# A 32-chunk recommender tower on one core: one more rolled copy of h in PSUM, six split pairs of tiles a chunk instead of five

## The chip, the cores and the metric

The kernel runs on one core of one Trainium2 chip. The metric is the device time of one launch in microseconds; lower is better. The engines have these names in the profile: PE is TensorE (PEld its weight loads), DVE is VectorE, ACT is ScalarE, POOL is GpSimd and SP is SyncE, which here only issues DMAs.

## The reference

The inputs are 1024 rows of 32 ids and 16 dense values. Each id picks a row of 32 numbers from its own table, which gives `x` of shape (1024, 32 fields, 32). A compressed interaction network with three layers works on `x`:

```
for i, (W, b) in enumerate(zip(Ws, bs)):
    z = einsum('bhd,bmd,ohm->bod', h, x, W.reshape(O, H, F))
    z = relu(z + b[None, :, None])
    if i < n_layers - 1: h, direct = z[:, :O//2], z[:, O//2:]
    else:                direct = z
out = sum over d of concat(directs)
```

Layer 0 has h = x (32 by 32 pairs of fields, 128 outputs), layer 1 has 64 by 32 pairs and 128 outputs, layer 2 has 64 by 32 pairs and one output. The 129 sums and the 16 dense values then pass through a small network (145 to 512 to 256 to 1, relu between). Everything is float32.

## The kernel before

The 1024 by 32 columns (sample, d) are cut into 32 chunks of 1024 columns. For a layer, each product h[i] * x[j] is a row, and 128 such rows are one tile, which PE multiplies by a 128 by 128 block of the weights. To make a tile, DVE multiplies h by x rolled over the partitions (`x_roll`, four shifts) or h rolled by 16 partitions a step (`h_roll`, entry 0 is h, entries 1 to 3 are copies rolled by one, two, three steps, made by DMAs). Tiles are made in pairs (128 by 2048 elements), one DVE instruction a pair. Layer 1 has 16 tiles, eight pairs.

A tile reaches PE in one of two ways. A **whole** pair is multiplied as float32 (eight matmul records of 512 columns). A **split** pair goes as two float32r parts: DVE makes the raw product (`raw`), ACT rounds it (`prod_hi`), and the remainder `raw - prod_hi` (`prod_lo`) is made by DVE (`split_rest`) or GpSimd; PE then runs hi*hi, hi*lo and lo*hi (twelve records a pair). A split begins only when its remainder is there.

Per chunk c before, layer 0 of the next chunk has two whole pairs, here called **W0a** and **W0b** on DVE and **L0a** and **L0b** on PE. Layer 1 has three whole pairs (R from `h_roll` entry 1, L1b and L1c from h itself) and five split pairs: B0, B1, B2, B3 (h rolled by two and three against x shift 0 to 3) and A1 (h rolled by one against x shifts 2 and 3). GpSimd makes the remainders of B1 and B3 and, between them, eight gathers of table rows (an indirect DMA each) for the chunk three ahead. DVE makes the remainders of B0, A1 and B2.

Five further pieces per chunk: `product16` and `split_rest16` (DVE) and two matmuls on PE make layer 0's pairs of fields 16 apart; ACT puts relu on layer 0 (`relu0`) and on layer 1 (`relu1`); `layer2_u` (PE) and `layer2` (DVE) make layer 2's product, and every fourth chunk `layer2_sum` (PE) adds four of them; `sum_direct` (DVE) sums layer outputs.

`mlp_ps` is one PSUM tile of 1024 columns. ACT copies the next chunk's x into it (`copy_x`), which W0a and W0b read, then h (`copy_h0`), which L1b and L1c read. So those four DVE products read PSUM and SBUF; the others read SBUF twice.

The order on each engine is written out by hand in its `step`, and engines meet only at semaphores. The whole products use a ring of two buffers (`prod`): the product number n waits until PE has used number n - 2 (`whole` in the vector block):

```
wait(dve, prod_used, n - RING + 1)
```

PE's order before is L0a, B3 of the chunk before, L0b, R, the 16-apart matmuls, `layer2_u`, B0, L1b, B1, L1c, A1, (`layer2_sum`), B2. In SP's step, the loads of `x_roll` for chunk c wait until the slot, last used by chunk c - 2, is free, and the three rolls of h of chunk c - 1 (`roll_h`, two DMAs each) stand between the second and the third of those loads.

Of the kernel before, what the change touches and what calls it, by code (L numbers as in the profile page):

```python
# [31 lines left out]
P = 128  # L32
# [100 lines left out]
def build_tower(nc, gather_ids, row_base, table, w0, w0_swapped, w1_whole, w1_split, w2, b0, b1, b2,  # L133
                dense_t, wt1a, wt1b, bt1, wt2, bt2, wt3, out):
    with ExitStack() as ctx:
# [39 lines left out]
        x_part16 = sb("x_part16", [P, 2, PART])  # L175
# [11 lines left out]
        h2 = sb("h2", [P, 2, BANK])  # L187
# [12 lines left out]
        mlp1_hi = prod_hi[:, 0:2, :, :].rearrange("p s k n -> p (s k) n")  # L200
        mlp1_lo = prod_lo[:, 0:2, :, :].rearrange("p s k n -> p (s k) n")
        wt2_hi = w1_hi[:, 0:M1 * TOP2 // P, :].rearrange("p t n -> p (t n)").rearrange("p (k n) -> p k n", n=TOP2)
        wt2_lo = w1_lo[:, 0:M1 * TOP2 // P, :].rearrange("p t n -> p (t n)").rearrange("p (k n) -> p k n", n=TOP2)
        mlp2 = x_roll[:, 0, 0:M2, :]
        wt2_sb = x_roll[:, 0, M2, :].rearrange("p (k n) -> p k n", n=TOP2)
        top_a_hi, top_a_lo = [prod_hi[:, SPLIT_SLOT[A1], k, :] for k in range(2)]
        top_b_parts = prod_lo[:, SPLIT_SLOT[A1], 0, :]
        wt1a_hi, wt1a_lo = [prod_lo[:, SPLIT_SLOT[A1], 1, k * TOP1:(k + 1) * TOP1] for k in range(2)]
# [21 lines left out]
        x_part16_loaded = [sem(f"x_part16_loaded{s}") for s in range(2)]  # L230
# [29 lines left out]
        lo1_ready = sem("lo1_ready")  # L260
# [79 lines left out]
        def _(pool):  # L340
# [14 lines left out]
            def gather(c, u, group, part):  # L355
# [6 lines left out]
                for g in range(part * GATHERS // 2, (part + 1) * GATHERS // 2):  # L362
# [6 lines left out]
            def lo1(c):  # L369

                rounded = settled(pool, c * SPLIT1 + B1 + 1)
                behind = settled(pool, lo_count(c, B0))
                pool.wait_ge(hi_ready, rounded)
                pool.wait_ge(lo_ready, behind)
                nc.gpsimd.tensor_tensor(prod_lo[:, SPLIT_SLOT[B1], :, :], raw[:, RAW_SLOT[B1], :, :],  # L375
                                        prod_hi[:, SPLIT_SLOT[B1], :, :], ALU.subtract).then_inc(lo1_ready, 1)

            def lo3(c):

                rounded = settled(pool, c * SPLIT1 + B3 + 1)  # L380
                behind = settled(pool, lo_count(c, B2))
                pool.wait_ge(hi_ready, rounded)
                pool.wait_ge(lo_ready, behind)
                nc.gpsimd.tensor_tensor(prod_lo[:, SPLIT_SLOT[B3], :, :], raw[:, RAW_SLOT[B3], :, :],  # L384
                                        prod_hi[:, SPLIT_SLOT[B3], :, :], ALU.subtract).then_inc(lo3_ready, 1)

            def step(c, u, group):
# [6 lines left out]
                more = not isinstance(c, int) or c + ahead < CHUNKS  # L394
                if more:
                    if u == 1:
                        make_rows(group + 1)
                    gather(c + ahead, (u + ahead) % UNROLL, group if u == 0 else group + 1, 0)
                lo1(c)
                if more:  # L400
                    gather(c + ahead, (u + ahead) % UNROLL, group if u == 0 else group + 1, 1)

            make_rows(0)
            for c in range(UNROLL - 1):
                for part in range(2):
                    gather(c, c, 0, part)
# [3 lines left out]
        def _(sp):  # L410
# [9 lines left out]
            def roll_h(c, s):  # L420

                sp.wait_ge(h1_ready, 2 * (c + 1))
                for a in range(1, ROLLS):
# [17 lines left out]
            def load_x(c, u):  # L441
# [16 lines left out]
                if is_first(c):  # L458
                    load_part16(c, s)
                if not isinstance(c, int) or c != 1:  # L460
                    load_base(c)
                for b in range(ROLLS):

                    if reuses:
                        sp.wait_ge(*free[b])
# [3 lines left out]
                    if b == 1:  # L469
# [6 lines left out]
                        if not is_first(c):  # L476
                            load_part16(c, s)
# [16 lines left out]
            sp.dma_start(wt2_sb, wt2).then_inc(mlp_loaded, 16)  # L494

# [10 lines left out]
        def _(dve):  # L506
# [22 lines left out]
            def product16(c, u, group):  # L529
                s = u % 2  # L530

                dve.wait_ge(gather_done[u], (group + 1) * (16 * GATHERS))
                dve.wait_ge(x_part16_loaded[s], (c - s + 2) * 8)
                wait(dve, twice16_ready, c * 64)
                nc.vector.tensor_tensor(raw16[:, :], gathered[:, u, :], x_part16[:, s, :], ALU.mult
                                        ).then_inc(raw16_ready, 1)

            def products0(c, u, group):
# [22 lines left out]
                if not is_first(c):  # L561
                    product16(c, u, group)

# [642 lines left out]
```

## Time and profile before

| What | us |
|---|---|
| median of 3 runs (1127.32 to 1129.06) | 1128.2 |
| the profiled execution's own time | 1127.21 |
| its span, first to last instruction | 1125.4 |
| PE busy | 1086.0 |
| DVE busy | 1034.8 |
| POOL busy | 744.1 |
| ACT busy | 597.8 |

The mean granted TensorE clock is 0.995. Busy PE is not PE at its peak: the ends of its records are modelled and overlap the next record's start, so the distance between two starts is the better measure. The steady part of the run, chunk after chunk, is nearly all of the span, so the period of one chunk times about thirty is the time.

### The profile page before, as it was taken

To read this page: it belongs to the slowest core of one execution; us is meant where nothing else is said; L and a number is where in the kernel's file an instruction comes from. 1 tells how busy PE (TensorE), PEld (TensorE's weight loads), DVE (VectorE), ACT (ScalarE), POOL (GpSimd) and SP (SyncE) were. 2 spreads that over 40 slices of the span, in tenths; PEclk is the share of its full clock that TensorE was granted. 3 is DMA by queue.
4 is the path that set the end of the run, shared out by engine and by line. 5 is a ranking of instruction groups with operands and counts; after the bars stand their busy time and mean duration, and the time that the engine had idled before them with its cause. 6 is when DMAs were issued, how large, how long until landed. Compare 5 with 4: busy or idle time off the path is not lost.

```text
span 1125.4 us, 11475 instructions
## 1 busy us (share of the span) xinstructions
PE 1086.0 (97%) x3562; PEld 660.5 (59%) x3562; DVE 1034.8 (92%) x580; ACT 597.8 (53%) x517; POOL 744.1 (66%) x333
## 2 busy tenths in 40 slices
PE   3789999999999999999999999999999999999997
PEld 1355655666565666656666666656665666656665
DVE  1589999999999999999999999999999999999993
ACT  0156555545654555565455556555545655555545
POOL 6466767777787777768777777877777787743110
PEclk9899999999999999999999999999999999999999
DMA  6665454665544466554446555544566554455200
GB/s 203 206 166 147 141 144 132 177 174 153 149 147 135 129 177 176 166 143 138 141 128 171 176 155 161 141 134 127 169 176 168 148 142 145 131 153 145 78 0 1
DMA packets 73576, 162.97 MB, mean 145 GB/s; under 512 B 14785, under 2 KB 39874, under 8 KB 73554
## 3 DMA queue, kind: packets, MB, share of 16 engines
q1 hardware_dynamic: 52738, 147.57, 46.2%
q10 hardware_dynamic: 12624, 10.92, 3.0%
q0 software_dynamic: 8192, 4.21, 2.3%
q8 instruction: 11, 0.18, 0.1%
q14 instruction: 11, 0.09, 0.0%
HBM read 95.52 MB, written 8.39 MB: 92 GB/s over the span
## 4 chain that ended last, share of the span: by engine, by line
PE 86%; DVE 6%; issue 2%; ACT 1%; DMA 1%; another core or an unknown queue 1%; ACTq 1%; POOL 1%; SPq 0%; DVEq 0%; POOLq 0%
PE z_ps L723 84%; DVE raw L591 2%; PE u_ps L723 2%; DVE prod L527 2%; DVE prod_lo L597 2%; DMA twice<-raw 1%; POOL gathered L364 1%; ACTq L1016 0%; ACT prod_hi L1097 0%; ACT h_roll L1083 0%; PE mlp_ps L723 0%; ACT h L969 0%; DMA gathered<-in_table,rows_sb 0%; DMA base_sb<-in_row_base 0%
## 5 line engine op out<-in xcount | busy, mean ns | idle before, releaser
L723 PE MATMUL z_ps<-prod,w_sb 128*128 128x512 f32 x1280 | 575.6, 596 | 10.8 <-ACT direct L959 4.0
L364 POOL DMA_INDIRECT gathered<-in_table,rows_sb x256 | 454.1, 1774 | 73.9 <-issue 68.3
L723 PEld LDWEIGHTS z_ps<-prod,w_sb 128*128 128x128 f32 x1280 | 243.6, 191 | 273.4 <-issue 262.3
L986 ACT CAST prod_hi<-raw 128x2048 fp32r<-128x2048 f32 x160 | 305.2, 1908 | 180.0 <-DVE raw L591 179.3
L591 DVE TENSOR_TENSOR raw<-h_roll,x_roll 128x2048 f32<-128x2048 f32 x160 | 363.4, 2288 | 1.2
L527 DVE TENSOR_TENSOR prod<-mlp_ps,x_roll 128x2048 f32<-128x2048 f32 x124 | 279.6, 2285 | 8.5 <-issue 5.7
L723 PE MATMUL z_ps<-prod_hi,w_hi 128*128 128x512 f32 x648 | 249.0, 464 | 3.5 <-DVE prod_lo L597 3.1
L375 POOL TENSOR_TENSOR prod_lo<-raw,prod_hi 128x2048 fp32r<-128x2048 f32 x32 | 146.8, 4587 | 135.4 <-DVE prod_lo L597 109.1
L597 DVE TENSOR_TENSOR prod_lo<-raw,prod_hi 128x2048 fp32r<-128x2048 f32 x98 | 223.9, 2286 | 1.0
L384 POOL TENSOR_TENSOR prod_lo<-raw,prod_hi 128x2048 fp32r<-128x2048 f32 x30 | 139.0, 4632 | 122.3 <-DVE prod_lo L597 122.3
L723 PE MATMUL z_ps<-prod_lo,w_hi 128*128 128x512 f32 x648 | 204.8, 396 | 0.0
L723 PE MATMUL z_ps<-prod_hi,w_lo 128*128 128x512 f32 x648 | 204.2, 395 | 0.0
L723 PEld LDWEIGHTS z_ps<-prod_hi,w_hi 128*128 128x128 f32 x648 | 121.4, 189 | 72.9 <-issue 47.8
L723 PEld LDWEIGHTS z_ps<-prod_hi,w_lo 128*128 128x128 f32 x648 | 121.6, 188 | 30.1
L723 PEld LDWEIGHTS z_ps<-prod_lo,w_hi 128*128 128x128 f32 x648 | 121.6, 188 | 29.4
L955 ACT ACTIVATE h_roll<-z_ps,b_sb 64x1024 f32<-64x1024 f32 x64 | 71.2, 1112 | 95.3 <-PE z_ps L723 84.1
L999 ACT COPY mlp_ps<-h_roll 128x1024 f32<-128x1024 f32 x32 | 32.6, 1017 | 130.6 <-DVE prod L527 130.6
L527 DVE TENSOR_TENSOR prod<-h_roll,x_roll 128x2048 f32<-128x2048 f32 x32 | 73.3, 2292 | 27.7 <-PE z_ps L723 20.9
L969 ACT ACTIVATE h<-z_ps,b_sb 64x512 f32<-64x512 f32 x64 | 43.6, 682 | 26.4 <-PE z_ps L723 25.5
L959 ACT ACTIVATE direct<-z_ps,b_sb 64x1024 f32<-64x1024 f32 x32 | 35.6, 1111 | 33.0 <-DVE top_a L612 29.4
L612 DVE TENSOR_REDUCE top_a<-direct 128x1024 f32 (+1 forms) x32 | 38.7, 1209 | 0.0
L973 ACT ACTIVATE direct<-z_ps,b_sb 64x1024 f32<-64x1024 f32 x32 | 35.5, 1109 | 0.8
(71 smaller groups left out, 329.5 us busy)
## 6 DMA issues: line engine op xcount, KB each, us to landing
x_roll<-x_dram SPq DMA_DIRECT2D x128, 512.0 KB
x_base<-x_dram SPq DMA_DIRECT2D x32, 512.0 KB
h_roll<-h_roll SPq DMA_DIRECT2D x32, 448.0 KB
h_roll<-h_roll SPq DMA_DIRECT2D x32, 384.0 KB
h_roll<-h_roll SPq DMA_DIRECT2D x32, 320.0 KB, 6.0
x_dram<-gathered SPq DMA_DIRECT2D x64, 128.0 KB
twice<-raw ACTq DMA_DIRECT2D x128, 64.0 KB
h_roll<-h_roll SPq DMA_DIRECT2D x32, 192.0 KB, 7.0
```

The costliest lines, as they stand in the source:

```text
L364: nc.gpsimd.indirect_dma_start(gathered[:, u, g * DIM:(g + 1) * DIM], None, table, bass.IndirectOffsetOnAxis(ap=rows_sb[:, col:col + 1], a ...
L375: nc.gpsimd.tensor_tensor(prod_lo[:, SPLIT_SLOT[B1], :, :], raw[:, RAW_SLOT[B1], :, :], prod_hi[:, SPLIT_SLOT[B1], :, :], ALU.subtract).th ...
L384: nc.gpsimd.tensor_tensor(prod_lo[:, SPLIT_SLOT[B3], :, :], raw[:, RAW_SLOT[B3], :, :], prod_hi[:, SPLIT_SLOT[B3], :, :], ALU.subtract).th ...
L527: nc.vector.tensor_tensor(prod[:, slot % RING, :, :], in0, in1, ALU.mult).then_inc(prod_ready, 1)
L591: nc.vector.tensor_tensor(raw[:, RAW_SLOT[r], :, :], hs, xs, ALU.mult).then_inc(raw_ready, 1)
L597: nc.vector.tensor_tensor(prod_lo[:, slot, :, :], raw[:, RAW_SLOT[r], :, :], prod_hi[:, slot, :, :], ALU.subtract).then_inc(lo_ready, 1)
L612: nc.vector.tensor_reduce(sums[:, :, bass.ds(group * rows, rows)], direct[:, u % 2, :].rearrange("p (q r d) -> p q r d", q=QUADS, d=DIM), ...
L723: return nc.tensor.matmul(*args, **kw)
L955: nc.scalar.activation(h_roll[half * HID:(half + 1) * HID, s, 0, :], z0_ps[0:HID, :], ACT.Relu, bias=b0_sb[0:HID, :]).then_inc(h1_ready, 1)
L959: nc.scalar.activation(direct[0:HID, s, :], z0_ps[HID:P, :], ACT.Relu, bias=b0_sb[HID:P, :]).then_inc(direct0_ready, 1)
L969: nc.scalar.activation(h2[half * HID:(half + 1) * HID, s, :], z1_of(c)[0:HID, half * BANK:(half + 1) * BANK], ACT.Relu, bias=b1_sb[0:HID, ...
L986: nc.scalar.copy(prod_hi[:, SPLIT_SLOT[r], :, :], raw[:, RAW_SLOT[r], :, :]).then_inc(hi_ready, 1)
```

## The change

Layer 1 has now two whole pairs and six split pairs. The whole pair R becomes the split pair A10 (h rolled by one against x shifts 0 and 1); A1 is now named A12. ACT copies the h rolled by one into `mlp_ps` (`copy_h1`, after the two whole products of layer 1 have read h there), and A10 and A12 read it from PSUM. Both whole products of layer 1, here **L1a** and **L1b**, are those that read h in `mlp_ps`.

GpSimd now makes three remainders per chunk, B3 of the chunk before, B0 and B2, with two, three and three gathers behind them. Each waits for a point in DVE's order as well as for its data (`window`): B3 for the remainder of A12, B0 for `product16`, B2 for `split_rest16`. DVE makes the remainders of B1, A10 and A12. There are three raw buffers (`RAW_RING`) instead of two.

The orders are written anew. DVE, step c: W0a, W0b (of c + 1), B0, B1, `product16`, L1a, L1b, `sum_direct`, B2, remainder of B1, `split_rest16`, A10, A12, `layer2`, B3, remainder of A10, remainder of A12. PE: L0a, B3 of c - 1, L0b, L1a, L1b, B0, the 16-apart matmuls, `layer2_u`, B1, B2, A10, (`layer2_sum`), A12. ACT: `copy_h0`, round B0, `relu1`, the four DMAs of `double_pairs16`, round B1, `copy_h1`, `round_pairs16`, round B2, round A10, `relu0`, round A12, `copy_x`, round B3, `copy_late`. SP: the three rolls of h stand behind all four loads of `x_roll`, in the order two, three, one; the loads wait for the raw products A10, A10, A12 and B3 of the chunk that used the slot. `x_part16` and `h2` have one buffer each, and two weights of the last network are loaded at the end, by SP, into `x_roll`.

```diff
-WHOLE1 = 3
-B0, B1, A1, B2, B3 = range(5)
-SPLIT1 = 5
+WHOLE1 = 2
+B0, B1, B2, A10, A12, B3 = range(6)
+SPLIT1 = 6
 RING = 2
-SPLIT_SLOT = (0, 1, 2, 0, 1)
+SPLIT_SLOT = (0, 1, 2, 0, 1, 2)
-RAW_SLOT = (0, 1, 0, 1, 0)
-RAW_RING = 2
-LO_ORDER = {B0: 1, A1: 2, B2: 3, B3: 4}
+RAW_SLOT = (1, 2, 0, 1, 2, 0)
+RAW_RING = 3
+LO_ORDER = {B1: 1, A10: 2, A12: 3, B3: 4}
...
+            def lo(c, r, window, opened, ready):
+                rounded = settled(pool, c * SPLIT1 + r + 1)
+                opened = settled(pool, opened)
                 pool.wait_ge(hi_ready, rounded)
+                pool.wait_ge(window, opened)
+                nc.gpsimd.tensor_tensor(prod_lo[:, SPLIT_SLOT[r], :, :], raw[:, RAW_SLOT[r], :, :],
+                                        prod_hi[:, SPLIT_SLOT[r], :, :], ALU.subtract).then_inc(ready, 1)
...
-                    lo3(c - 1)
+                    lo(c - 1, B3, lo_ready, lo_count(c - 1, A12), lo3_ready)
+                    gather(*after, range(0, 2))
-                lo1(c)
+                    lo(c, B0, raw16_ready, c + 2, lo0_ready)
+                    gather(*after, range(2, 5))
+                    lo(c, B2, lo16_ready, c + 2, lo2_ready)
+                    gather(*after, range(5, GATHERS))
...
(SP, load_x)
+                    free = [settled(sp, (c - 2) * SPLIT1 + r + 1) for r in (A10, A10, A12, B3)]
...
-                        if reuses:
-                            roll_h(c - 1, 1 - s)
+                if reuses:
+                    roll_h(c - 1, 1 - s)
...
(DVE, split_product)
+                if r == A10:
+                    dve.wait_ge(h1_copied, c + 1)
+                    dve.wait_ge(lo0_ready, c + 1)
+                elif r == A12:
+                    dve.wait_ge(lo_ready, lo_count(c, B1))
+                elif r == B3:
+                    dve.wait_ge(lo2_ready, c + 1)
...
+                if r in (A10, A12):
+                    k = PAIR * (r - A10)
+                    hs, xs = twice(mlp_ps[:, :]), x_roll[:, s, k:k + PAIR, :]
...
(ACT)
+            def copy_h1(c, u):
+                s = u % 2
+                act.wait_ge(h1_rolled[s][0], (c - s + 2) * 16)
+                act.wait_ge(prod_ready, first1(c) + WHOLE1)
+                nc.scalar.copy(mlp_ps[:, :], h_roll[:, s, 1, :]).then_inc(h1_copied, 1)
...
-                act.wait_ge(prod_ready, first1(c - 2) + WHOLE1)
+                act.wait_ge(raw_ready, (c - 2) * SPLIT1 + A12 + 1)
                 nc.scalar.copy(mlp_ps[:, :], x_base[:, :]).then_inc(x_copied, 1)
```

## Rows read from the trace of the kernel before

**Rows 1.** The page's first part: engine, busy us (share of span), instructions.
```profile
PE 1086.0 (97%) x3562; PEld 660.5 (59%) x3562; DVE 1034.8 (92%) x580; ACT 597.8 (53%) x517; POOL 744.1 (66%) x333
```

**Rows 2.** Waits of DVE: engine and line, released by, us in total, times, longest.
```profile
DVE prod L527 <- PE z_ps L723: 21.5, 18, 5.4
```

**Rows 3.** Timeline of PE: start us, us, engine, line, operation, out<-in, shape, count.
```profile
676.81 1.03 PE L723 MATMUL z_ps<-prod_hi,w_hi 128*128 128x512 f32 x2
...
680.01 7.03 PE L723 MATMUL z_ps<-prod,w_sb 128*128 128x512 f32 x16
686.47 1.04 PE L723 MATMUL z_ps<-hi_lo,w_sb 128*128 128x512 f32 x2
...
703.49 0.62 PE L723 MATMUL z_ps<-prod_hi,w_hi 128*128 128x512 f32 x2
...
706.29 3.60 PE L723 MATMUL z_ps<-prod,w_sb 128*128 128x512 f32 x8
709.32 1.03 PE L723 MATMUL z_ps<-prod_hi,w_hi 128*128 128x512 f32 x2
```

**Rows 4.** Timeline of DVE over one chunk; brackets: idle before, and releaser.
```profile
689.61 1.21 DVE L612 TENSOR_REDUCE top_a<-direct 128x1024 f32 x1
...
701.87 4.60 DVE L527 TENSOR_TENSOR prod<-mlp_ps,x_roll 128x2048 f32<-128x2048 f32 x2
706.39 0.63 DVE L535 TENSOR_TENSOR raw<-gathered,x_part 128x256 f32<-128x256 f32 x1
...
709.92 2.29 DVE L527 TENSOR_TENSOR prod<-h_roll,x_roll 128x2048 f32<-128x2048 f32 x1 [0.70 <-issue]
...
714.45 0.69 DVE L568 TENSOR_TENSOR hi_lo<-twice,hi_lo 64x512 fp32r<-64x512 f32 x1
...
717.38 4.50 DVE L527 TENSOR_TENSOR prod<-mlp_ps,x_roll 128x2048 f32<-128x2048 f32 x2
721.79 0.41 DVE L605 TENSOR_TENSOR h2x<-u_ps,x_late 128x256 f32<-128x256 f32 x1
722.12 1.21 DVE L612 TENSOR_REDUCE top_a<-direct 128x1024 f32 x1
723.25 4.48 DVE L591 TENSOR_TENSOR raw<-h_roll,x_roll 128x2048 f32<-128x2048 f32 x2
```

**Rows 5.** Timeline of DVE: the sums of the outputs in steps 1 and 30.
```profile
100.63 1.21 DVE L612 TENSOR_REDUCE top_a<-direct 128x32 f32<-128x1024 f32 x1
...
1049.64 1.21 DVE L612 TENSOR_REDUCE top_a<-direct 128x32 f32<-128x1024 f32 x1
```

**Rows 6.** Timeline of DVE early on: a remainder that PE waits for.
```profile
76.15 2.28 DVE L597 TENSOR_TENSOR prod_lo<-raw,prod_hi 128x2048 fp32r<-128x2048 f32 x1
```

**Rows 7.** Timeline of PE there: the split that waited, and what follows it.
```profile
78.48 0.73 PE L723 MATMUL z_ps<-prod_hi,w_hi 128*128 128x512 f32 x2 [0.29 <-DVE prod_lo L597]
...
81.40 3.60 PE L723 MATMUL z_ps<-prod,w_sb 128*128 128x512 f32 x8
```

**Rows 8.** Timeline of ACT in the same chunk.
```profile
687.55 2.25 ACT L955 ACTIVATE h_roll<-z_ps,b_sb 64x1024 f32<-64x1024 f32 x2 [2.90 <-PE z_ps L723]
690.86 1.11 ACT L959 ACTIVATE direct<-z_ps,b_sb 64x1024 f32<-64x1024 f32 x1 [1.06 <-DVE top_a L612]
...
697.07 1.01 ACT L1005 COPY mlp_ps<-x_base 128x1024 f32<-128x1024 f32 x1
699.79 1.91 ACT L986 CAST prod_hi<-raw 128x2048 fp32r<-128x2048 f32 x1 [1.70 <-DVE raw L591]
```

**Rows 9.** Timeline of POOL: the two remainders of that stretch.
```profile
702.10 4.64 POOL L384 TENSOR_TENSOR prod_lo<-raw,prod_hi 128x2048 fp32r<-128x2048 f32 x1 [3.86 <-DVE prod_lo L597]
...
717.61 4.58 POOL L375 TENSOR_TENSOR prod_lo<-raw,prod_hi 128x2048 fp32r<-128x2048 f32 x1 [2.37 <-DVE prod_lo L597]
```

**Rows 10.** The rolls of h (line 425): issue to landing.
```profile
DMA to landing us min/median/max: 5.2/6.0/7.0
```

**Rows 11.** Busy time of a ten-us stretch with those rolls; last three: clock, DMA share, GB/s.
```profile
590.00:600.00 10.00, 10.00 (x36) 6.50 (x35) 9.96 (x7) 7.53 (x7) 8.87 (x5) 1.00 1.01 256
```

More of the change, by code:

```diff
@@ L229, in build_tower @@
         x_base_loaded = sem("x_base_loaded")
-        x_part16_loaded = [sem(f"x_part16_loaded{s}") for s in range(2)]
+        x_part16_loaded = sem("x_part16_loaded")
         x_roll_loaded = [[sem(f"x_roll_loaded{s}_{b}") for b in range(ROLLS)] for s in range(2)]
@@ L361, in gather @@
                 wait(pool, late_copied, freed)
-                for g in range(part * GATHERS // 2, (part + 1) * GATHERS // 2):
+                for g in columns:
                     col = u * GATHERS + g
@@ L391, in step @@
                 if not_first(c) and pool_makes_lo3(c - 1 if isinstance(c, int) else c):
-                    lo3(c - 1)
+                    lo(c - 1, B3, lo_ready, lo_count(c - 1, A12), lo3_ready)
                 ahead = UNROLL - 1
                 more = not isinstance(c, int) or c + ahead < CHUNKS
+                after = c + ahead, (u + ahead) % UNROLL, group if u == 0 else group + 1
                 if more:
@@ L422, in roll_h @@
                 sp.wait_ge(h1_ready, 2 * (c + 1))
-                for a in range(1, ROLLS):
+                for a in (2, 3, 1):
                     r = H_ROLL * a
@@ L628, in step @@
                 before = (u - 1) % UNROLL, group if u else group - 1
-                def rolled_once():
-                    dve.wait_ge(h1_ready, 2 * (c + 1))
-                    dve.wait_ge(h1_rolled[s][0], (c - s + 2) * 16)
-                    whole(first1(c), slot1(c, u), twice(h_roll[:, s, 1, :]), x_roll[:, s, 0:PAIR, :])
-                if is_first(c):
-                    rolled_once()
                 split_product(c, u, B0)
-                if not is_first(c):
-                    rolled_once()
                 split_product(c, u, B1)
                 if not is_last(c):
-                    split_rest16(c + 1)
-                split_rest(c, B0)
+                    product16(c + 1, (u + 1) % UNROLL, group if u < UNROLL - 1 else group + 1)
                 dve.wait_ge(h0_copied, c + 1)
                 for k in range(PAIRS0):
-                    whole(first1(c) + 1 + k, slot1(c, u) + 1 + k, twice(mlp_ps[:, :]),
+                    whole(first1(c) + k, slot1(c, u) + k, twice(mlp_ps[:, :]),
                           x_roll[:, s, k * PAIR:(k + 1) * PAIR, :])
                 if not_first(c):
+                    sum_direct(c - 1, *before)
+                split_product(c, u, B2)
+                split_rest(c, B1)
+                if not is_last(c):
+                    split_rest16(c + 1)
+                split_product(c, u, A10)
+                split_product(c, u, A12)
+                if not_first(c):
                     layer2(c - 1, *before)
-                    sum_direct(c - 1, *before)
-                split_product(c, u, A1)
-                split_product(c, u, B2)
-                split_rest(c, A1)
                 split_product(c, u, B3)
-                split_rest(c, B2)
+                split_rest(c, A10)
+                split_rest(c, A12)
                 if not pool_makes_lo3(c):
@@ L1027, in step @@
                     copy_h0(c, u)
+                round_products(c, B0)
+                if not_first(c):
+                    relu1(c - 1, (u - 1) % UNROLL)
                 if not is_last(c):
                     double_pairs16(c + 1)
-                round_products(c, B0)
+                round_products(c, B1)
+                copy_h1(c, u)
                 if not is_last(c):
                     round_pairs16(c + 1)
-                if not_first(c):
-                    relu1(c - 1, (u - 1) % UNROLL)
-                round_products(c, B1)
+                round_products(c, B2)
+                round_products(c, A10)
                 if not is_last(c):
                     relu0(c + 1, (u + 1) % UNROLL)
-                round_products(c, A1)
-                if not is_last(c):
-                    copy_late(c + 1, (u + 1) % UNROLL, group if u < UNROLL - 1 else group + 1)
-                round_products(c, B2)
+                round_products(c, A12)
                 if not isinstance(c, int) or c + 2 < CHUNKS:
@@ L1044, in step @@
                 round_products(c, B3)
+                if not is_last(c):
+                    copy_late(c + 1, (u + 1) % UNROLL, group if u < UNROLL - 1 else group + 1)
                 if u == 0 and not_first(c):
@@ L1160, in lay_out @@
     w1 = a["L0_rec_W1"].reshape(P, HID, FIELDS)
[L1161 to L1162 removed]
+    whole = [(0, 0), (0, 1), (0, 2), (0, 3)]
+    split = [(2, 0), (3, 0), (2, 1), (3, 1), (2, 2), (3, 2), (1, 0), (1, 1), (1, 2), (1, 3), (2, 3), (3, 3)]
     for name, tiles in (("w1_whole", whole), ("w1_split", split)):
```

142 lines of the change are left out of this document (62 added, 80 removed).

## The prediction

> **What bounds the kernel now.** I read the busy shares first: PE 97%, DVE 92%, the others far lower [rows 1]. So two engines are near full, and a gain on one is capped by the other. Next the timeline of PE in the middle of the run: each record starts before the one ahead has ended, with no idle time. Then DVE over the same chunk: it is full but for one gap before R, the whole product behind B0 [rows 4]. It is DVE that waits for PE there: L0a starts at 706.29 [rows 3], and R at 709.92 [rows 4], 3.63 us later, when PE gives the ring's buffer back; the waits by releaser say the same, 21.5 us in 18 such waits [rows 2]. PE is the bound. A chunk takes 32.51 us (722.12 - 689.61, rows 4); every fourth one has `layer2_sum` as well, and the mean over 29 periods is (1049.64 - 100.63)/29 = 32.72 [rows 5].
>
> **PE's own work.** A whole pair is priced from starts: L0b and R together take 6.46 us from start to start (680.01 to 686.47) and a single one ahead of a split 3.03 (706.29 to 709.32), so a further whole pair is worth 3.43; a further split pair is 2.80 (703.49 to 706.29) [rows 3]. One pair goes from whole to split, so PE saves 0.63 us a chunk, if nothing else ends later.
>
> **DVE's work.** It loses R and one remainder (GpSimd makes three now, not two) and gains the raw product A10 and the remainder of A10; A1 and B2 stay in other places. Thirteen instructions of 2048 columns before, thirteen after. A10 and A12 read PSUM in place of SBUF: two products with a PSUM input take 4.50, two with SBUF inputs 4.48 [rows 4]. So nothing is gained or lost in DVE's work, about 31.8 a chunk (32.51 less the gap of 0.70).
>
> **The loop that the new order closes.** L1b on DVE takes the ring's buffer that W0b filled, so it waits until PE has done L0b. In the old order the product behind L0b had 7 us of other work ahead of it; the one that waits sooner, R, waits only for L0a. In the new order PE reaches L0b only after A10, A12, L0a and B3, and A10 waits for the last remainder but one that DVE makes. This is one loop, once a chunk, and no engine can run ahead in it:
>
> DVE, from the start of L1b to the end of A10's remainder: L1b 2.21 (half of 4.41, 717.38 to 721.79), `sum_direct` 1.13 (722.12 to 723.25), B2 2.21, a remainder and `split_rest16` 2.93 (714.45 to 717.38), A10 and A12 4.41, `layer2` 0.33 (721.79 to 722.12), B3 2.21 [rows 4], the remainder 2.28 [rows 6]: 17.71.
>
> DVE to PE: the remainder that PE waited for ended at 76.15 + 2.28 = 78.43 [rows 6], and the split began at 78.48 [rows 7]: 0.05.
>
> PE, from A10 to the release of L1b: A10, a split that has waited, 2.92 (78.48 to 81.40) [rows 7]; A12 2.80; L0a 3.03; B3 behind it 3.20 (676.81 to 680.01); L0b until DVE goes on 3.63, as for R above [rows 3, 4]: 15.58.
>
> Sum 33.34. Inside it B3 on DVE also waits for GpSimd's remainder of B2, whose raw buffer it takes. That remainder starts 0.23 after the first of two products that read PSUM (717.38 on DVE, 717.61 on POOL) and takes 4.58 to 4.64, so it ends 4.81 to 4.87 after A10's start [rows 4, 9]; DVE is at B3 after 4.41 + 0.33 = 4.74. That adds 0.1 to 0.2: 33.5 us. The same loop in the old order, R to B2's remainder to B2, L0a and R, is 24.46 (32.51 less 8.05, the way from W0a to R in rows 4) + 0.05 + 2.92 + 3.63 = 31.06, and so had 1.45 to spare under 32.51.
>
> **The sum.** `layer2_sum` stands between A10 and A12 and so in the loop; it costs what it did, 0.21 a chunk on the mean (32.72 - 32.51). New mean 33.71, against 32.72: 0.99 a chunk. L1b waits for an L0b in steps 1 to 30, which makes 29 periods: 28.7 us. Against the profiled execution's 1127.2 that is 1155.9; the median of the runs lies 1.0 above that execution, so 1157. The first step and the end I leave at nothing: DVE makes the same number of instructions there, and the two weights now loaded late land long before the last network needs them. If that cover is gone they cost their own few us.
>
> **Edits that I cost at nothing.** ACT has one round more (1.91) and one copy more (1.01) a chunk [rows 8]; its 597.8 us of busy time [rows 1] rise by 32 x 2.92 = 93 to some 690, so there is room on the mean. Its order: round A10 is ready 10.76 + 1.91 = 12.7 after L1b's start, and DVE wants it at 15.4; `copy_h1` needs L1b's end and is wanted by A10 6.3 later, behind `sum_direct`, B2, a remainder and `split_rest16`. GpSimd: three remainders are 13.9 and eight gathers of 1.77 with 0.3 between them about 16.6, together 30.5 of 33.5. Without that cover, B3 on DVE waits longer and each us of it is a us of the loop. Loads of `x_roll` now start behind A10 and not behind L1b; the first has from there to W0a, about 10 us. The rolls of h, six DMAs, pass two loads on SP's queue and are priced under the rivals; the store of the next chunk's gathered rows, queued behind them, serves a chunk two steps ahead. With one `x_part16` its load waits for `product16` of the chunk before, a step earlier; with one `h2`, `relu1` waits for a `layer2_u` a step earlier: both are long past.
>
> **The port that DVE and GpSimd share.** The trace shows little of it: GpSimd's remainder ends at 702.10 + 4.64 = 706.74 [rows 9], and the small `product16`, with two SBUF inputs, started at 706.39, takes 0.63 instead of about 0.4 [rows 4]. The Trainium skill, in "SBUF — State Buffer", section "SBUF: two separate sides", says that a VectorE instruction with two SBUF inputs and a GpSimd instruction that reads SBUF exclude each other for the whole instruction. By that rule a late remainder of B3 on GpSimd would hold up B0 on DVE altogether; row and rule agree in direction, and how long a large product is held no row shows. This is a loop of its own, priced from rows: L1b to the end of A10 10.76; on ACT round A10 1.91, `relu0` 2.25 + 1.11, round A12 1.91, `copy_x` 1.01, round B3 1.91, together 10.10 [rows 8]; GpSimd 0.2 + 4.64 [rows 9]; DVE's B0, B1, `product16` and L1a 7.05: 32.75. It is shorter than 33.5, so it is not added.
>
> **The rivals.**
>
> *PE stays the bound.* The period would be 32.51 - 0.63 = 31.88, the mean 32.09, and the time 1127.2 - 0.63 x 29 = 1109. For it: PE is at 97%, DVE has 0.70 of slack, and the work of both fits. Against it: the loop is made only of waits that stand in the code and of durations in rows. It decides only if PE runs L0b more than 1.6 us sooner after A10's remainder than rows 3 and 7 show.
>
> *The loop through ACT and GpSimd sets the period, with the first loop shorter than I think.* Then 32.75 + 0.21 = 32.96, and 0.24 x 29 = 7 more: 1134. If both loops come out 0.3 shorter there is no change, 1128. For it: the exclusion above; against it: the first loop is longer by 0.75.
>
> *Something is late inside the loop, so that it is slower still.* Two candidates. ACT: if its row of five is 1 us longer than 10.10 plus the 0.75 in hand, or GpSimd comes late to B2's remainder because its three gathers run long. DMA: the rolls of h, behind all loads now, are wanted by B0. From A10's end six transfers of 0.52 MB and one of 0.13 must pass, at 256 GB/s with the DMA engines full [rows 11] 12.8 us; with the landing of a roll 6.0 (5.2 to 7.0) from its issue [rows 10] they come about 25 after L1b's start, and 25 + 7.05 = 32.1 against 33.5. Roughly 1 us more in the loop is 29 us: 1186; half that, 1171.
>
> **How the numbers follow.** The forecast, loop of 33.2 to 33.8: 1148 to 1166, chance 0.62. Something late inside: 1166 to 1190, 0.18. The second loop or a shorter first one: 1126 to 1148, 0.10, of which 0.04 within 0.2% (2.3 us, about what a measurement of this kernel can tell). PE the bound: 1105 to 1126, 0.10. So faster 0.10, same 0.04, slower 0.86. The range 1138 to 1182 leaves out the PE bound, half of the third case and the top of the second, about 0.18.
>
> **What would show it.** Right: DVE idles before L1b and not before R's place, released by PE, some 0.5 to 1.5 us a chunk; PE idles 1.2 to 1.6 us before A10, released by DVE's remainder (line 597 of before); the start of `sum_direct` repeats every 33.5 us. Wrong: PE without idle time before A10 means the loop is not closed; idle time of DVE before B3 (released by GpSimd) or before B0 (by a DMA) means the third rival; a large product on DVE beginning only when GpSimd's remainder ends would show the exclusion. The forecast falls if the period is under 33.

## The result, and the profile after

| | before | after |
|---|---|---|
| median of the runs, us | 1127.8 (4 runs, 1126.6 to 1129.1) | 1178.6 (4 runs, 1175.5 to 1181.3) |
| profiled execution, us | 1127.2 | 1175.5 |
| its span, us | 1125.4 | 1173.7 |
| mean granted TensorE clock | 0.995 | 0.989 |

The ratio is 1.045, with a 95% interval of 1.042 to 1.048: the change makes the kernel slower by 51 us. The forecast was 1157, and its range reached from 1138 to 1182. The sign and the place of the first loss are as forecast, and a second loss of some 20 us came on top, so that the time lies where the forecast's third rival put it (1166 to 1190).

The page's first part after (engine, busy us, share of the span, instructions), to be held against [rows 1]:

```profile
PE 1082.3 (92%) x3690; PEld 682.7 (58%) x3690; DVE 1036.8 (88%) x580; ACT 691.3 (59%) x581; POOL 921.1 (78%) x365
```

PE and DVE do what they did, within 4 us, in a span that is 48 us longer: neither has more to do, both wait more. (ACT and POOL have more to do, but are busy for 59% and 78% of the span.) For what PE and DVE wait is in the waits by releaser of the kernel after (engine, line, released by, us in total, times, longest). First DVE, the answer to [rows 2], then PE, and last the same wait of PE in the kernel before:

```profile
DVE raw L594 <- DMA h_roll<-h_roll: 39.6, 25, 3.7
DVE prod L530 <- PE z_ps L721: 12.0, 15, 1.1
...
PE z_ps L721 <- DVE prod_lo L600: 35.8, 30, 1.5
...
PE z_ps L723 <- DVE prod_lo L597: 3.1, 4, 1.6
```

PE now waits 1.2 us a chunk for a remainder of DVE (35.8 in 30), which before it did four times in the run. DVE waits for PE less often than before, and the largest entry is new: B0 waits for the rolls of h.

The timeline of DVE after, one chunk (start, us, operation; brackets: idle time before, and releaser), with the first and the thirtieth sum of outputs ahead of and behind it:

```profile
94.81 1.21 DVE L615 TENSOR_REDUCE top_a<-direct 128x32 f32<-128x1024 f32 x1
...
544.16 1.21 DVE L615 TENSOR_REDUCE top_a<-direct 128x1024 f32 x1
...
573.54 4.48 DVE L530 TENSOR_TENSOR prod<-mlp_ps,x_roll 128x2048 f32<-128x2048 f32 x2
577.94 1.21 DVE L615 TENSOR_REDUCE top_a<-direct 128x1024 f32 x1
...
584.30 4.49 DVE L594 TENSOR_TENSOR raw<-mlp_ps,x_roll 128x2048 f32<-128x2048 f32 x2
...
596.13 4.58 DVE L530 TENSOR_TENSOR prod<-mlp_ps,x_roll 128x2048 f32<-128x2048 f32 x2
...
603.00 4.49 DVE L594 TENSOR_TENSOR raw<-h_roll,x_roll 128x2048 f32<-128x2048 f32 x2 [2.28 <-DMA h_roll<-h_roll]
...
607.74 4.48 DVE L530 TENSOR_TENSOR prod<-mlp_ps,x_roll 128x2048 f32<-128x2048 f32 x2
612.14 1.21 DVE L615 TENSOR_REDUCE top_a<-direct 128x1024 f32 x1
...
1089.54 1.21 DVE L615 TENSOR_REDUCE top_a<-direct 128x32 f32<-128x1024 f32 x1
```

The mean over 29 periods is (1089.54 - 94.81)/29 = 34.30, against 32.72 in [rows 5]: 1.58 x 29 = 45.8 of the 48.3 us between the two profiled executions. The other 2.5 are the start (94.81 against 100.63, 5.8 sooner) and the end (1173.7 - 1089.54 = 84.2 against 75.8, 8.4 longer). Much of these two is only where the mark stands: `sum_direct` comes 16.0 behind W0a now (596.13 to 612.14) and came 20.25 behind it before (701.87 to 722.12) [rows 4]. Single periods are uneven: 33.78 (544.16 to 577.94), 34.20 (577.94 to 612.14); over the 29 they go from 33.46 to 35.44, and none is shorter. So there is a floor at the forecast's 33.5, and something that adds to it in most chunks.

What adds is the gap before B0. L1b starts at 573.54 + 2.24 = 575.78, the rolls are there at 603.00: 27.2 us later, where the forecast had 25. From B0 to the next L1b are 607.74 + 2.24 - 603.00 = 6.98, and 27.2 + 7.0 = 34.2 is this period.

PE of the same chunk, from the split A10 that waited (its first record, then those of A12, L0a, B3 and L0b):

```profile
593.63 0.73 PE L721 MATMUL z_ps<-prod_hi,w_hi 128*128 128x512 f32 x2 [0.90 <-DVE prod_lo L600]
...
596.54 0.62 PE L721 MATMUL z_ps<-prod_hi,w_hi 128*128 128x512 f32 x2
...
599.34 3.60 PE L721 MATMUL z_ps<-prod,w_sb 128*128 128x512 f32 x8
602.37 1.03 PE L721 MATMUL z_ps<-prod_hi,w_hi 128*128 128x512 f32 x2
...
605.57 3.59 PE L721 MATMUL z_ps<-prod,w_sb 128*128 128x512 f32 x8
```

The steps are 2.91, 2.80, 3.03 and 3.20: the forecast's terms to 0.01, out of [rows 3, 7].

Why the rolls land late is read from SP's queue (the issues) and from the busy time by stretches (last three columns: clock, DMA share, GB/s), both of the kernel after:

```profile
586.62 1.34 SPq L468 DMA_DIRECT2D x_roll<-x_dram  x2
...
588.95 3.13 SPq L468 DMA_DIRECT2D x_roll<-x_dram  x2
592.20 0.61 SPq L426 DMA_DIRECT2D h_roll<-h_roll  x1
...
594.78 0.60 SPq L427 DMA_DIRECT2D h_roll<-h_roll  x1
```

```profile
586.00:588.00 2.00, 2.00 (x11) 1.68 (x10) 2.00 (x2) 1.37 (x1) 2.00 (x1) 1.00 0.00 0
588.00:592.00 4.00, 4.00 (x19) 3.23 (x18) 4.00 (x4) 3.90 (x5) 3.85 (x2) 1.00 1.01 336
...
596.00:602.00 6.00, 6.00 (x23) 3.88 (x22) 4.71 (x3) 1.97 (x3) 5.82 (x3) 1.00 1.02 216
588.00:602.00 14.00, 13.10 (x52) 9.32 (x51) 12.36 (x7) 9.87 (x9) 13.06 (x6) 1.00 1.00 264
602.00:604.00 2.00, 2.00 (x9) 1.30 (x8) 1.00 (x1) 0.00 (x0) 1.70 (x2) 1.00 0.34 83
```

The loads start when A10 is done (586.5) and the rolls follow the fourth load, which waits for B3. The forecast let 3.3 MB flow at 256 GB/s from A10's end. The rate is about right: from 588 to 602 the DMA engines are full, at 264 GB/s on the mean. But nothing moves until 588, 1.5 us behind A10's end, and more than 3.3 MB passes: 264 x 14 and 83 x 2 are 3.9 MB by 604, which takes in all three rolls. The roll by one stands last on the queue and is wanted much later than B0; it is out from 595.4 on, so its 0.52 MB move beside the rolls that B0 wants. Four loads, the load for `product16` and three rolls are 3.8 MB, 14.8 us at 256 GB/s, and 586.5 + 1.5 + 14.8 = 602.8, against 603.0 (an estimate from these rows; no run leaves out the roll by one).

The last of the four roll DMAs that B0 wants is out at 595.4, and B0 starts 7.6 us later. [rows 10] has the first of the two DMAs of each roll (line 425); those that B0 waits for last are the second ones (line 426 of before), and they took longer in the old order too:

```profile
DMA to landing us min/median/max: 5.5/7.0/8.8
```

### The profile page after: what moved, and what is told of

The parts are those of the page before. It is cut to its first block, busy times and chain, and to the rows that moved or that the text cites. A ratio compares the mean times of both kernels' runs of the same rounds, so it can differ in the third digit from the quotient of the medians.

```text
span 1173.7 us, 12034 instructions
## 1 busy us (share of the span) xinstructions
PE 1082.3 (92%) x3690; PEld 682.7 (58%) x3690; DVE 1036.8 (88%) x580; ACT 691.3 (59%) x581; POOL 921.1 (78%) x365
## 4 chain that ended last, share of the span: by engine, by line
DVE 30%; PE 24%; issue 16%; DMA 8%; POOL 8%; SPq 3%; ACT 2%; DVEq 1%; ACTq 0%; POOLq 0%
PE z_ps L721 24%; DVE raw L594 16%; DMA h_roll<-h_roll 8%; DVE prod_lo L600 7%; POOL prod_lo L376 5%; POOL gathered L365 4%; DVE prod L530 3%; DVE top_a L615 2%; SPq L426 2%; SPq L468 1%; SPq L427 1%; DVE h2x L608 1%; DVE raw L537 0%; ACT h_roll L951 0%; PE mlp_ps L721 0%
## 5 line engine op out<-in xcount | busy, mean ns | idle before, releaser
L982 ACT CAST prod_hi<-raw 128x2048 fp32r<-128x2048 f32 x192 | 366.1, 1907 | 287.8 <-DVE raw L594 245.2
L376 POOL TENSOR_TENSOR prod_lo<-raw,prod_hi 128x2048 fp32r<-128x2048 f32 x94 | 431.8, 4594 | 124.0 <-DVE raw L537 63.4
L721 PE MATMUL z_ps<-prod,w_sb 128*128 128x512 f32 x1024 | 463.2, 603 | 25.1 <-DVE prod L530 16.3
L721 PEld LDWEIGHTS z_ps<-prod,w_sb 128*128 128x128 f32 x1024 | 195.6, 193 | 259.0 <-issue 228.9
L594 DVE TENSOR_TENSOR raw<-h_roll,x_roll 128x2048 f32<-128x2048 f32 x128 | 295.2, 2326 | 54.3 <-DMA h_roll<-h_roll 39.6
L721 PE MATMUL z_ps<-prod_hi,w_hi 128*128 128x512 f32 x776 | 280.0, 441 | 42.2 <-DVE prod_lo L600 35.8
L721 PE MATMUL z_ps<-prod_lo,w_hi 128*128 128x512 f32 x776 | 244.6, 395 | 0.0
L721 PE MATMUL z_ps<-prod_hi,w_lo 128*128 128x512 f32 x776 | 244.4, 395 | 0.0
L594 DVE TENSOR_TENSOR raw<-mlp_ps,x_roll 128x2048 f32<-128x2048 f32 x64 | 143.6, 2286 | 0.9
L998 ACT COPY mlp_ps<-h_roll 128x1024 f32<-128x1024 f32 x32 | 32.5, 1017 | 116.3 <-DVE prod L530 116.3
L1005 ACT COPY mlp_ps<-h_roll 128x1024 f32<-128x1024 f32 x32 | 32.5, 1016 | 12.9 <-DVE prod L530 12.6
```

Of the source, the lines that this page charges most:

```text
L376: nc.gpsimd.tensor_tensor(prod_lo[:, SPLIT_SLOT[r], :, :], raw[:, RAW_SLOT[r], :, :], prod_hi[:, SPLIT_SLOT[r], :, :], ALU.subtract).then_ ...
L594: nc.vector.tensor_tensor(raw[:, RAW_SLOT[r], :, :], hs, xs, ALU.mult).then_inc(raw_ready, 1)
L721: return nc.tensor.matmul(*args, **kw)
L982: nc.scalar.copy(prod_hi[:, SPLIT_SLOT[r], :, :], raw[:, RAW_SLOT[r], :, :]).then_inc(hi_ready, 1)
```

## The experiments

| run | us | ratio to before, 95% interval | period, us |
|---|---|---|---|
| the change | 1178.6 | 1.042 to 1.048 | 33.5 to 35.4 |
| e1 early h | 1153.6 | 1.021 to 1.030 | 33.61 |
| e2 row numbers in two pieces | 1173.0 | 1.037 to 1.049 | uneven |
| e3 both | 1154.6 | 1.021 to 1.031 | 33.61 |
| e8 two half loads | 1158.3 | 1.025 to 1.032 | 33.47 |
| e4 A10's remainder first | 1191.6 | 1.055 to 1.066 | uneven, 35 |
| e5 e3 and A10's remainder first | 1146.5 | 1.014 to 1.021 | 33.31, about a fourth 34.1 to 34.6 |
| e6 rolls ahead of two loads | 1281.8 | 1.131 to 1.142 | uneven, 37.9 |
| e7 e6, row numbers, `relu0` first | 1235.6 | 1.091 to 1.101 | uneven, 36.2 |
| e10 e3, all loads half | 1155.0 | 1.021 to 1.031 | 33.61 |
| e9 e10, A10's remainder first | 1151.6 | 1.019 to 1.029 | 33.32, half 34.1 |
| e12 e10, half remainders on GpSimd | 1150.4 | 1.019 to 1.027 | 33.42 |
| e11 e12, A10's remainder first | 1141.4 | 1.012 to 1.020 | 33.31 |

Each has 4 runs, beside the kernel before on the same chip. A period is that of a plain chunk; in e1, e3, e8, e10 and e12 a chunk with `layer2_sum` is 0.76 or 0.77 longer. All start from the change. All but e2, e4, e6 and e7 leave out a part of what the kernel must compute (B0 to B2 read h where they should read its rolled copies, loads move half of their columns, or GpSimd makes half of its remainders) and serve for times alone.

**e1 and e8: are the rolls the second loss, and is it bandwidth?** e1 takes the wait away, e8 leaves the wait and takes bytes out ahead of it.

```diff
                 if r == B0:
+                    dve.wait_ge(h1_ready, 2 * (c + 1))
+                if r == B3:
                     for a in range(PAIR, ROLLS):
                         dve.wait_ge(h1_rolled[s][a - 1], (c - s + 2) * 16)
...
-                    hs, xs = h_roll[:, s, PAIR:2 * PAIR, :], twice(x_roll[:, s, b, :])
+                    hs = twice(h_roll[:, s, 0, :]) if r < A10 else h_roll[:, s, PAIR:2 * PAIR, :]
+                    xs = twice(x_roll[:, s, b, :])
```

> The changed kernel, but B0, B1 and B2 multiply h itself (entry 0) instead of the copies rolled by two and three, so that DVE does not wait for those DMAs before B0; all rolls are still moved, and B3 still reads two of them. Theory (two loops: the ring's loop closes at 33.48 us, and late rolls lengthen it to 34.2 in most chunks): the wait of DVE for the DMA of h (39.6 us in all) goes, chunks of 33.48 become the rule, about 1160 against 1178.6; the chunks in which GpSimd is late remain. Rival (the rolls are only in front of some other wait, of ACT or GpSimd, of the same length): no change, 1175 to 1180. Rival (the ring's loop does not hold, PE is the bound): about 1110.

Measured: 1153.6. Its waits of DVE and of PE, the lines that carry them:

```profile
DVE prod L530 <- PE z_ps L724: 38.9, 31, 1.9
...
PE z_ps L724 <- DVE prod_lo L603: 46.0, 32, 1.5
```

No wait of DVE for a DMA of h is left, and what stands in its place is what the forecast named: L1b waits for PE 1.25 us in each chunk, A10 on PE waits 1.44 for DVE's remainder. The rolls cost 25.0 us (1178.6 - 1153.6).

```diff
+                    cols = CHUNK // 2 if reuses and b >= 2 else CHUNK
...
-                                  [[CHUNK, FIELDS], [x_shift(1, 0) * CHUNK, QUADS], [1, CHUNK]])
+                                  [[CHUNK, FIELDS], [x_shift(1, 0) * CHUNK, QUADS], [1, cols]])
...
```

> The changed kernel, but from chunk 2 on the third and fourth load of x_roll move only the first 512 of 1024 columns (the rest keeps older x), 0.52 MB less of the 3.3 MB between A10 and B0. Theory that the rolls are late for want of bandwidth (216 to 289 GB/s with the DMA engines at 100%): they land 2 us or more earlier, and the time falls to 1155 to 1163. Rival (their issue or a fixed latency makes them late): 1174 to 1179.

Measured: 1158.3, with DVE's wait for the rolls down from 39.6 to 8.8 us. Three sums of outputs of this run, two plain chunks and then one with `layer2_sum`:

```profile
531.32 1.21 DVE L616 TENSOR_REDUCE top_a<-direct 128x1024 f32 x1
564.79 1.21 DVE L616 TENSOR_REDUCE top_a<-direct 128x1024 f32 x1
598.25 1.21 DVE L616 TENSOR_REDUCE top_a<-direct 128x1024 f32 x1
632.47 1.21 DVE L616 TENSOR_REDUCE top_a<-direct 128x1024 f32 x1
```

Periods of 33.47, 33.46 and 34.22: with 0.5 MB a chunk less ahead of the rolls the period falls to the floor and stays there. The order is untouched, and so is the moment of issue. In the second of these chunks the last roll DMA that B0 wants (SP's queue) and B0 (DVE) are

```profile
581.37 0.60 SPq L427 DMA_DIRECT2D h_roll<-h_roll  x1
```

```profile
587.72 5.11 DVE L595 TENSOR_TENSOR raw<-h_roll,x_roll 128x2048 f32<-128x2048 f32 x2 [0.27 <-DMA h_roll<-h_roll]
```

The DMA is out 19.4 behind the start of L1b, as in the change (19.6), and B0 starts 5.75 later in place of 7.6. So the rolls are late for want of bandwidth, and 33.47 is the ring's loop. (e1 is 4.7 us faster at a longer period. In the profiled executions, 3.0 apart, its first sum is at 89.1 and that of e8 at 92.8, as its first B0 waits for no rolls; its 29 periods take 3.0 longer, and its end is 2.3 shorter.)

**e2 and e3: GpSimd's row numbers.** In the change GpSimd waited up to 2.6 us for its own gathers to land, before it made row numbers. They are made in two pieces here, so that none waits for the last gathers.

```diff
...
-                        make_rows(group + 1)
+                        make_rows(group + 1, range(0, UNROLL - 1))
+                    if u == 2:
+                        make_rows(group + 1, range(UNROLL - 1, UNROLL))
...
```

> The changed kernel, but GpSimd makes the row numbers for the gathers in two pieces: three quarters in the second chunk of a group, which no longer wait for the gathers just issued, and the last quarter one chunk later. Theory that GpSimd's wait there (11.6 us in all, up to 2.6 each) makes its remainders of B0 and B2 late in one chunk of four, so that DVE waits at B3 (1.17 each): 7 chunks of 35.3 shorten by 0.8 to 1.2, 1169 to 1173. Rival (late rolls fill the place of that wait at once): 1176 to 1179.

> Both of the former: B0, B1 and B2 read h itself, and the row numbers are made in two pieces. Theory: only the ring's loop is left, 33.48 a chunk and 0.77 more in every fourth, which is the forecast of 33.7 on the mean: 1155 to 1159. Rival (a third loop, ACT's five pieces and GpSimd's remainder of B3 with the shared port): 34 or more, 1165 and up. Rival (PE is the bound once the DMA is out of the way): 1110.

Measured: 1173.0, 5.6 us under the change with intervals that overlap, and 1154.6 with early h against 1153.6 without. In e2 the wait for the rolls grew from 39.6 to 50.3 us: what one wait gave back the other took. With the rolls out of the way the row numbers are worth nothing.

**e4 and e5: A10's remainder ahead of B3.** If the ring's loop goes through A10's remainder, taking one instruction of 2.2 us from in front of it must shorten that loop.

```diff
+                split_rest(c, A10)
                 split_product(c, u, B3)
-                split_rest(c, A10)
```

> The changed kernel, but DVE makes the remainder of A10 ahead of the raw product B3, which takes one instruction (2.2 us) out of the ring's loop and puts B3, and with it the last load of x_roll and the rolls behind it, 2.2 us later. If late rolls set the period: slower, up to 2 us a chunk, 1200 to 1235. If the ring's loop alone sets it: faster, 31.3 in the loop, so PE and the rest set the period, 1115 to 1140. Equal shares: 1170 to 1185.

> Run e3 (B0, B1 and B2 read h itself, row numbers in two pieces) with the remainder of A10 made ahead of the raw product B3. Theory: e3 stands at 33.61 a chunk because of the ring's loop, and this takes 2.2 us out of it; then PE (32.1 on the mean), DVE (about 31.8) or the last load of x_roll, which B3 now holds up 2.2 us longer, sets the period: 1110 to 1135, under the 1127.6 of the kernel before if PE sets it. Rival (something else closes at 33.6, the ring's wait only sits in front of it): 1150 to 1156.

Measured: e4 1191.6, slower than the change by 13 us, between the two bands that were expected. B3 comes later, the fourth load and the rolls behind it too, and DVE's wait for the rolls grows to 59.6 us (26 times): in the kernel as it is, the rolls set the period. e5 gives 1146.5, under the rival's band and far above the theory's, and 33.31, so turning the order is worth 0.30 a chunk and not 2.2. DVE waited there 24.6 us for the last load of `x_roll`, and I took that load for the next loop; e9 tests it.

**e6 and e7: an order of SP that was to bring the rolls in time.** Rolls two and three go ahead of loads three and four; e7 also lets `relu0` go before A10's round and has the row numbers of e2.

```diff
...
                     if b == 1:
+                        if reuses:
+                            roll_h(c - 1, 1 - s, (2, 3))
...
-                    roll_h(c - 1, 1 - s)
+                    roll_h(c - 1, 1 - s, (1,))
```

> The changed kernel, but the rolls of h by two and three stand between the second and the third load of x_roll on SP's queue, as all rolls did in the kernel before; the roll by one stays last. Theory that the place in the queue makes the rolls late: DVE's waits for them (39.6 us) go, 1155 to 1162. Rival that the bytes do (four loads and the rolls all start after A10, 3.3 MB with the DMA engines full): the last loads of x_roll are late in their place and W0b waits for them, 1170 to 1185.

> e6, and with it the row numbers in two pieces, and ACT's relu0 ahead of the rounding of A10, so that the rolls can start some 2 us earlier. If the place and the start decide: the ring's loop only, 1153 to 1158. If the bytes decide: some of it, 1160 to 1175. It would not beat the kernel before in either case.

Measured: 1281.8 and 1235.6, both far above every expectation. In e6 (SP's queue, then DVE) the rolls wait for `relu0`, and loads three and four, which could have gone at 600 and 602.6, wait behind them on the queue:

```profile
602.13 0.61 SPq L426 DMA_DIRECT2D h_roll<-h_roll  x1
...
606.05 1.73 SPq L468 DMA_DIRECT2D x_roll<-x_dram  x2
```

```profile
577.90 2.29 DVE L532 TENSOR_TENSOR prod<-mlp_ps,x_roll 128x2048 f32<-128x2048 f32 x1 [6.16 <-DMA x_roll<-x_dram]
```

The second row is W0b of the chunk before, where it was the same: W0b wants the last load before B0 wants the rolls, and waits up to 6.2 us. What was overlooked in both theories is that an order on one queue also passes on the waits of what stands first.

**e9 and e10: are the loads the next loop?** Both are e3 with all four loads cut to 512 of their 1024 columns (the expectation says 2048, which is wrong); e9 turns the order as well.

```diff
+                    cols = CHUNK // 2 if reuses else CHUNK
...
```

> Leaves out: B0, B1 and B2 read entry 0 of h in place of the rolled copies, and from the third chunk on each of the four x_roll loads moves 512 of its 2048 columns. So neither the rolls nor the loads can be late. What is left is the ring's loop of the forecast, 33.5 us a chunk (33.47 measured with the loads 3 and 4 cut), and TensorE's 32.1 under it. Theory (the ring's loop sets the period by itself): 33.5 to 33.6 a chunk as in the run with early h and full loads, 1150 to 1157 us. Rival (some transfer still stood in those runs' loop): under 33.2 a chunk, below 1146.

> As the kernel beside it (entry 0 of h read by B0 to B2, loads of 512 columns), and A10's remainder stands ahead of B3's on VectorE. The theory's ring loop then loses one remainder of 2.24 us: 33.5 - 2.2 = 31.3, which is under TensorE's own work of about 32.1 a chunk, so TensorE sets the period: (32.1 - 33.6) x 29 = -43 from its neighbour, 1107 to 1118 us, below the kernel before (1127.7). Rival 1: ScalarE and GpSimd close a loop of about 32.7 to 32.8 (the price of the exclusive port in the forecast): 1125 to 1135. Rival 2: the order on VectorE doesn't matter for the loop: within 3 us of its neighbour.

Measured: e10 1155.0 and 33.61, the ring's loop alone, as expected. e9 1151.6, a miss: DVE's wait for `x_roll` is gone (1.6 us in all), and plain chunks stay at 33.32. My reading of e5 falls; the load was only the one that came last, at the same moment as something else. GpSimd's timeline in e9 over one chunk looked like that something:

```profile
589.93 4.57 POOL L378 TENSOR_TENSOR prod_lo<-raw,prod_hi 128x2048 fp32r<-128x2048 f32 x1
594.66 0.95 POOL L367 DMA_INDIRECT gathered<-in_table,rows_sb  x1 [0.16 <-issue]
595.92 2.65 POOL L367 DMA_INDIRECT gathered<-in_table,rows_sb  x1 [0.30 <-issue]
598.88 1.90 POOL L367 DMA_INDIRECT gathered<-in_table,rows_sb  x1 [0.30 <-issue]
600.82 4.62 POOL L378 TENSOR_TENSOR prod_lo<-raw,prod_hi 128x2048 fp32r<-128x2048 f32 x1
```

There is no idle time but that of issue, from chunk to chunk: GpSimd is full, three remainders and eight gathers (between 300 and 1000 us it is busy for 654, and 0.3 of issue stands ahead of most gathers).

**e11 and e12: GpSimd with room.** As e9 and e10, but in the steady chunks GpSimd makes half of each remainder.

```diff
+                n = PAIR if isinstance(c, int) else 1
-                nc.gpsimd.tensor_tensor(prod_lo[:, SPLIT_SLOT[r], :, :], raw[:, RAW_SLOT[r], :, :],
+                nc.gpsimd.tensor_tensor(prod_lo[:, SPLIT_SLOT[r], 0:n, :], raw[:, RAW_SLOT[r], 0:n, :],
```

> As the kernel beside it, with half remainders on GpSimd, but with the order of the change on VectorE (B3's product ahead of A10's remainder). Theory (the ring's loop of the forecast sets the period, and GpSimd only adds the 0.1 to 0.2 that B3 waits for it): 33.3 to 33.5 a chunk, 1146 to 1154 us, some 38 above its neighbour, which differs in this order alone. Rival (the period of 33.5 was GpSimd's and the shared port's from the start, and the ring's loop a thing that ran beside it): both fall alike, 1106 to 1120.

> Leaves out: B0, B1 and B2 read entry 0 of h in place of the rolled copies, each x_roll load moves 512 of its 1024 columns, and in the steady chunks GpSimd makes only half of each of its three remainders. A10's remainder stands ahead of B3's product. The neighbour with whole remainders on GpSimd repeats every 33.32 us with GpSimd without a gap (remainders 13.8, eight gathers of 1.98 with 0.3 between them, the rest row numbers), so neither PE nor the ring can show there. Theory (GpSimd was the bound of that run, and the forecast's ring loop is 31.2 to 31.3 with the order turned): GpSimd's row falls by some 6.9 us, PE's own work of 31.9 (32.1 with layer2_sum) sets the period, (32.1 - 33.5) x 29 = -41 from 1151.6: 1106 to 1116 us, below the kernel before. Rival: something other than GpSimd holds the period at 33.3: 1140 to 1152.

Measured: e12 1150.4 and 33.42, as the theory says: with GpSimd relieved the period stays that of the ring's loop. e11 1141.4 and 33.31 in every chunk from the third on, a miss again, in the rival's band: GpSimd, though full in e9, only added the 0.8 in half of the chunks there, and something else holds 33.31. What that is can be walked in e11. The three timelines are those of DVE (from one L1b to the next; the last bracket names no releaser), ACT and PE of the same chunk:

```profile
586.64 2.29 DVE L537 TENSOR_TENSOR prod<-mlp_ps,x_roll 128x2048 f32<-128x2048 f32 x1 [1.45 <-PE z_ps L731]
...
595.21 4.49 DVE L604 TENSOR_TENSOR raw<-mlp_ps,x_roll 128x2048 f32<-128x2048 f32 x2
...
604.83 2.29 DVE L610 TENSOR_TENSOR prod_lo<-raw,prod_hi 128x2048 fp32r<-128x2048 f32 x1 [0.40 <-ACT prod_hi L992]
...
619.95 2.29 DVE L537 TENSOR_TENSOR prod<-mlp_ps,x_roll 128x2048 f32<-128x2048 f32 x1 [1.49 <-issue]
```

```profile
597.54 1.91 ACT L992 CAST prod_hi<-raw 128x2048 fp32r<-128x2048 f32 x1 [3.34 <-DVE raw L604]
599.48 2.25 ACT L961 ACTIVATE h_roll<-z_ps,b_sb 64x1024 f32<-64x1024 f32 x2
601.75 1.12 ACT L965 ACTIVATE direct<-z_ps,b_sb 64x1024 f32<-64x1024 f32 x1
602.89 1.91 ACT L992 CAST prod_hi<-raw 128x2048 fp32r<-128x2048 f32 x1
```

```profile
605.93 0.64 PE L731 MATMUL z_ps<-h2x,quad_ones 128*32 128x256 f32 x8
607.18 0.73 PE L731 MATMUL z_ps<-prod_hi,w_hi 128*128 128x512 f32 x2 [0.61 <-DVE prod_lo L610]
...
616.32 9.17 PE L731 MATMUL z_ps<-prod,w_sb 128*128 128x512 f32 x21
```

L1b at 586.64, A10 done at 597.4, on ACT round A10, `relu0` (two parts), round A12 to 604.80, A12's remainder on DVE to 607.12, A12, L0a, B3 and L0b on PE, the next L1b at 619.95: 33.31. It is the same ring, closed over ACT and A12's remainder in place of DVE and A10's. `layer2_sum` (605.93) stands ahead of A12 on PE, off this way, which is why e11 has no longer chunk. In the change the two ways lie side by side, 33.4 and 33.3, so shortening one alone gives 0.1 to 0.3. That both must be shortened to see PE's 0.63 is argued from this walk; `relu0` behind A12's round, with the order turned, was not run, and stays open.

No run points to a version faster than the kernel before: the lowest, 1141.4, leaves work out and is still above it.

## Why the prediction was right, and where it was off

**PE's own work.** The steps of PE after are those of [rows 3, 7], so the price of a split pair holds. That PE saves 0.63 a chunk no run shows, as none has PE without a wait.

**DVE's work.** Right: 1034.8 became 1036.8 us, and a pair of products takes 4.48 to 4.58 with PSUM and 4.49 without.

**The ring's loop.** Right, in place and size: 33.34 worked out, 33.42 measured with GpSimd light (e12), 33.47 (e8) and 33.61 (e1, e3, e10) with GpSimd whole, against 33.5 forecast. Its two signs are there in e1, 1.25 us before L1b and 1.44 before A10. What was not seen is the second way round through ACT. The forecast priced ACT's row only towards GpSimd and B0 (32.75), not towards A12's remainder, which is 10.76 + 1.91 + 2.25 + 1.11 + 1.91 + 2.28 + 0.05 + 2.92 + 3.03 + 3.20 + 3.63 = 33.05 from the same rows, and 33.31 with the gaps. That cost the forecast nothing, but the expectations of e5, e9 and e11 fell by it.

**`layer2_sum`.** 0.21 a chunk forecast, 0.77/4 = 0.19 measured.

**B3 behind GpSimd.** 0.1 to 0.2 forecast; whole remainders against half ones are worth 0.19 a chunk (33.61 in e10 less 33.42 in e12).

**The rolls of h.** This is the step that failed, and it is one of size. The forecast saw the loop (landing, then B0 to L1b), gave it 25 + 7.05 = 32.1 and put it under the ring's 33.5, with a third rival, chance 0.18, in case it was late. It was: 27.2 + 7.0 = 34.2. The rate of 256 GB/s [rows 11] held (264). What was too small is what it was used on, and the landing: the sum of 3.3 MB leaves out the roll by one (0.52 MB, 2.0 us at 256 GB/s) and the 1.5 us in which nothing moves; and the 6.0 of [rows 10] is for a DMA that B0 does not wait for last, where the second ones have 7.0 in the same trace. These are two ways to see the same 2.1 us and do not add up; how they share it no run separates. The ring left 33.5 - 32.1 = 1.4 us for such an error, and it was 2.1. Cost: 20.3 us by e8, 25.0 by e1; the forecast is 21.6 below the median. That the time lies inside the range is no merit of the main sum: the forecast's own band ended at 1166, and the range held because it took in half of the third rival's.

**The start and the end.** Left at nothing; they were -5.8 and +8.4, of which some 4 each way is the place of `sum_direct` in the step, and 2.6 together. No experiment was made for them, and their cause stays open.

**The port that DVE and GpSimd share.** The sign named is there. In e9, with DVE's and GpSimd's timelines,

```profile
583.63 5.48 DVE L603 TENSOR_TENSOR raw<-h_roll,x_roll 128x2048 f32<-128x2048 f32 x2
```

```profile
580.15 4.59 POOL L378 TENSOR_TENSOR prod_lo<-raw,prod_hi 128x2048 fp32r<-128x2048 f32 x1
```

B0 and B1 take 5.48 in place of 4.48: GpSimd's remainder ended at 584.74, 1.11 into them, and they are 1.00 longer. It is as if a product that reads SBUF twice did not begin until GpSimd's remainder ends. This agrees with the exclusive lock that the Trainium skill states in "SBUF — State Buffer", section "SBUF: two separate sides".

## What to carry to other kernels

A chunk's order on several engines closes loops, and each loop's length is a sum that can be read off the old trace before the change is built; write down all ways from one waiting instruction back to itself, as two of them may be equal, and then no single cut shows. When transfers are moved behind others, price them by all bytes that are under way until they land, those queued behind them too, by the moment at which the first byte moves, and by the landing row of the very DMA that the consumer waits for last; then ask which consumer is left without slack. An order on one DMA queue also hands on the waits of its first transfer, which can cost more than the bytes.

## What the runs showed of the hardware that was not expected

The same gather issue on GpSimd takes 0.95 us or 1.9 to 3.0, and it goes with what DVE does beside it: in e9 the one at 594.66 (0.95) runs beside DVE's `sum_direct`, the one at 595.92 (2.65) beside B2's product, which reads SBUF twice. The mean gather goes from 1.62 us (e10) to 1.98 (e9) with nothing but the order of DVE changed, and eight of them by 2.8 us a chunk; with half remainders (e12, e11) the same turn leaves it at 1.31 and 1.33. So GpSimd's row is no fixed sum: 30.5 us a chunk in the forecast, without a gap at 33.3 in e9.

The DMA engines, full in both cases, moved 336 GB/s while only loads were out (588 to 592 in the kernel after) and 216 in the stretch of the rolls of h, SBUF to SBUF (596 to 602).
